# One power for queries and keys in two transformers, the first FFN's rounding done inside its attention, and a reordered layer norm after the recurrence

## The reference

```python
# layer 0, FFN: both operands of each product are rounded to FP4 in blocks of 16
scale = max(|xb|) / 6; scale = max(scale, 1e-12)
q = nearest_of_grid(xb / scale) * scale
gate = q(xn) @ q(w_gate).T ; up = q(xn) @ q(w_up).T
y = q(silu(gate) * up) @ q(w_down).T

# layers 2 and 3, FFN branch: a transformer of its own
# (layer 2: 6 layers, 16 heads, window 32; layer 3: 2 layers, 8 heads, window 64)
q = q / max(norm(q), 1e-12) * q_scale     # per head of 64, the same for k
q = rotate(q); k = rotate(k)
o = softmax(q k^T, banded) v
x = x + o @ wo ; x = x + w2(a * gelu(g)), a, g = split(w1(layernorm(shift(x))))

# layer 3, attention branch: a linear recurrence y, then
s = (y - mean) * rsqrt(var + eps) * gamma + beta
```

## Time and profile before

| | us |
|---|---|
| median of 3 runs | 4119.81 (4113.49 to 4121.21) |
| the profiled execution | 4123.83 |
| its span in the trace | 4122.1 |
| busy in the span: PE, DVE, ACT, POOL | 3719.1, 2877.2, 2448.5, 2308.0 |
| mean granted TensorE clock, share of full speed | 0.963 |

### The profile page before, as it was taken

How to read it: one execution, slowest core, us unless ns; L and a number is a source line. 1 busy time by engine, 2 the same in 40 slices (tenths; PEclk the granted TensorE clock), 3 DMA queues, 4 the chain that set the end, 5 groups by cost and what they waited for, 6 DMA issues and landing times. The chain is left out here.

```text
span 4122.1 us, 101183 instructions
## 1 busy us (share of the span) xinstructions
PE 3719.1 (90%) x40355; PEld 2527.8 (61%) x40365; DVE 2877.2 (70%) x6487; ACT 2448.5 (59%) x4999; POOL 2308.0 (56%) x2225
## 2 busy tenths in 40 slices
PE   7976999998999979999999999999999998768886
PEld 5554555544666646666666666666666666646665
DVE  3347454412666658888888888888888887558885
ACT  2223555523455557777767776777777776447775
POOL 1004000001111268888888888888888886257773
PEclk9997999998999989999999999999999999889998
DMA  0000000000000021112112112112111111120110
GB/s 20 2 8 23 1 1 1 6 24 7 2 2 2 2 79 41 41 41 67 41 41 67 41 41 67 41 41 67 41 41 38 41 41 33 34 69 23 24 24 19
DMA packets 103248, 128.53 MB, mean 31 GB/s; under 512 B 38232, under 2 KB 55680, under 8 KB 101888
## 3 DMA queue, kind: packets, MB, share of 16 engines
q1 hardware_dynamic: 102784, 122.05, 11.0%
HBM read 31.95 MB, written 3.54 MB: 9 GB/s over the span
## 5 line engine op out<-in xcount | busy, mean ns | idle before, releaser
L404 POOL TENSOR_TENSOR t_inv<-t_ssq,half 128x8 f32<-128x8 f32 x448 | 779.8, 1743 | 82.7 <-DVE t_ssq L682 62.5
L455 PE MATMUL t_wa<-t_w_qkv,t_resid 128*128 128x512 f32 x1344 | 694.4, 616 | 45.4 <-DMA t_scales<-in_L_ffn_k_scale 41.4
L415 POOL TENSOR_TENSOR t_ra<-t_qn,t_rot 128x512 f32<-128x512 f32 x448 | 570.3, 1273 | 85.1 <-DVE t_qn L689 76.7
L606 ACT ACTIVATE t_p<-t_p 128x384 f32<-128x384 f32 (+1 forms) x448 | 241.8, 540 | 331.2 <-DVE t_p L706 322.4
L715 DVE TENSOR_TENSOR t_ra<-t_ra,t_rb 128x512 f32<-128x512 f32 x448 | 311.0, 716 | 123.0 <-POOL t_rb L417 123.0
L484 PEld LDWEIGHTS t_T<-ident,t_p 128*96 128x96 f32 (+1 forms) x1792 | 193.1, 129 | 313.8 <-ACT t_p L606 280.4
L416 POOL TENSOR_TENSOR t_rb<-t_qn,t_rot 128x256 f32<-128x256 f32 x448 | 367.3, 820 | 0.0
L417 POOL TENSOR_TENSOR t_rb<-t_qn,t_rot 128x256 f32<-128x256 f32 x448 | 335.4, 749 | 0.0
L680 DVE TENSOR_REDUCE t_ssq<-t_sq 128x8 f32<-128x512 f32 x448 | 304.9, 681 | 12.0 <-ACT t_sq L598 8.2
L455 PEld LDWEIGHTS t_wa<-t_w_qkv,t_resid 128*128 128x128 f32 x1344 | 212.5, 192 | 163.2 <-issue 133.1
L492 PE MATMUL t_T<-ident,t_ra 128*128 128x128 f32 x1792 | 267.6, 277 | 44.0 <-ACT t_gg L645 32.4
(11 more groups left out here) (408 smaller groups left out, 8381.8 us busy)
## 6 DMA issues: line engine op xcount, KB each, us to landing
t_v<-t_vn SPq DMA_DIRECT2D x192, 198.0 KB, 2.6
t_v<-t_vn SPq DMA_DIRECT2D x248, 132.0 KB, 2.4
t_v<-t_vn SPq DMA_DIRECT2D x144, 66.0 KB, 1.9
t_w_qkv<-in_L_ffn_Wqkv SPq DMA_DIRECT2D x6, 1536.0 KB, 6.7
t_v<-t_nothing SPq DMA_DIRECT2D x48, 66.0 KB, 1.9
t_w_o<-in_L_ffn_Wo SPq DMA_DIRECT2D x6, 512.0 KB
f_h<-t_L_ffn_h_w SPq DMA_DIRECT2D x2, 1024.0 KB, 8.2
t_w<-in_L_ffn_W SPq DMA_DIRECT2D x6, 341.0 KB
```

The lines of the kernel that those rows point to most:

```text
L404: pool.tensor_tensor(inv[:, n % 2, r, :], ssq[:, n % 2, r, :], g["half"][:, 0:8], ALU.pow).then_inc(inved.sem, 1)
L415: pool.tensor_tensor(ra[:, n % 2, r], qn[:, r], spread(cos, 1, 8), ALU.mult).then_inc(cosd.sem, 1)
L455: pe.matmul(bank, resid[:, b, lo:lo + P], w_qkv[:, l % 2, at:at + 512], start=True, stop=True).then_inc(wa_up.sem, 1)
```

## The change

Three places. In `transformer` the floor and the power are done once for queries and keys, on 16 columns, after the keys' sums:

```diff
-        floored = st.event("floored", 2)
-        inved = st.event("inved", 2)
+        floored = st.event("floored")
+        inved = st.event("inved")
...
-                        for r in range(2):
-                            pool.wait_ge(floored.sem, floored.at(n, r + 1))
-                            pool.tensor_tensor(inv[:, n % 2, r, :], ssq[:, n % 2, r, :], g["half"][:, 0:8], ALU.pow).then_inc(inved.sem, 1)
+                        pool.wait_ge(floored.sem, floored.at(n))
+                        pool.tensor_tensor(inv[:, n % 2].rearrange("p r h -> p (r h)"), ssq[:, n % 2].rearrange("p r h -> p (r h)"), g["half"][:, 0:16],
+                                           ALU.pow).then_inc(inved.sem, 1)
...
                     v.tensor_reduce(ssq[:, n % 2, r, :], sq[:, r], X, ALU.add).then_inc(summed.sem, 1)
-                    v.wait_ge(summed.sem, summed.at(n, r + 1))
-                    v.tensor_scalar(ssq[:, n % 2, r, :], ssq[:, n % 2, r, :], 1e-24, None, ALU.max).then_inc(floored.sem, 1)
+                    if r:
+                        both = ssq[:, n % 2].rearrange("p r h -> p (r h)")
+                        v.wait_ge(summed.sem, summed.at(n, 2))
+                        v.tensor_scalar(both, both, 1e-24, None, ALU.max).then_inc(floored.sem, 1)
...
-                    v.wait_ge(inved.sem, inved.at(n, r + 1))
+                    v.wait_ge(inved.sem, inved.at(n))
```

```diff
+                    for k in ((0, 1, 2), (4, 5, 6))[half]:
+                        finish_rounding(k)
                     for b in range(NB):
+                        if half == 0 and b == 1:
+                            finish_rounding(3)
...
                             maxima(n + 2, 0)
+                            for i in range(PER_UNIT):
+                                round_step(PER_UNIT * (half * UNITS + n + 2) + i)
                             maxima(n + 2, 1)
...
-    parts = {"x0": (0, 512), "x1": (512, 512), "wgu": (WGU, 2 * NH * DIM), "wd": (WD, HID), "x2": (1024, 512), "x3": (1536, 512)}
-    for k in range(UNITS):
-        parts[f"h{k}"] = (HD + 2 * k * HID, 2 * HID)
...
-                for name, (lo, size) in parts.items():
+                for k in range(UNITS):
+                    lo, size = 2 * k * HID, 2 * HID
```

In `attention3`'s layer norm all four groups are measured first, their statistics counted four tiles ahead, and POOL takes the four powers in a row before the four additions of beta:

```diff
-                for i in range(T):
-                    v.bn_stats(stats[:, i, :], y[:, i, :]).then_inc(counted.sem, 1)
-                for k in range(6):
+                count_four(0)
+                for k in range(4):
+                    if k < 3:
+                        count_four(k + 1)
+                    measure(k)
+                for k in range(5):
                     if k < 4:
-                        measure(k)
-                    if 1 <= k < 5:
-                        shift(k - 1)
-                    if k >= 2:
-                        scale(k - 2)
+                        shift(k)
+                    if k:
+                        scale(k - 1)
```

More of the change, by code:

```diff
@@ L797, in attention0 @@
     loaded = early.loaded
-    wraw, wgraw, wv, wgv, wr, wo, gw, maskq, maskk, masklq, masklk = early.weights
+    wraw, wgraw, wv, wgv, wr, wo, gw, maskq, maskk, masklq, masklk, wff = early.weights
+    BL, HID, WGU = 16, 352, 3 * DIM
+    flat = lambda t, b: t[:, b * TPB:(b + 1) * TPB, :].rearrange("p t c -> p (t c)")
+    parts = [(flat(g["xn"], b), flat(g["u"], b)) for b in range(BATCH)]
+    parts += [(wff[:, lo:hi], wff[:, lo:hi]) for lo, hi in ((0, WGU), (WGU, 2 * WGU), (2 * WGU, 2 * WGU + HID))]
+    widths = [SEQ] * BATCH + [WGU, WGU, HID]
+    constants = flat(s, BATCH - 1)
+    blocks = lambda ap: ap.rearrange("p (k e) -> p k e", e=BL)
+    ROUND_STEPS, PER_UNIT = 7, 3
     with Stage(nc, "a0", early.sems) as st:
+        scale = st.sb("scale", [P, len(parts), SEQ // BL])
+        inverse = st.sb("inverse", [P, SEQ // BL])
+        r_stepped = st.sem("r_stepped")
+        r_lessened = st.sem("r_lessened")
         wqk = st.sb("wqk", [P, 2, G, 4, 32])
@@ L862, in _ @@
                 pool.memset(oE[:, :, :], 0.0)
-                pool.memset(oF[:, :, :], 0.0)
+                pool.memset(oF[:, :, :], 0.0).then_inc(zeroed, 1)
+                pool.wait_ge(zeroed, 12)
+                for k in range(2):
+                    pool.memset(wff[HID % P:P, (k + 1) * WGU - DIM:(k + 1) * WGU], 0.0)
             @block.sync
@@ L1309, in _, with ffn0 @@
                             gate_remote(b)
-def ffn0(nc, g, d):
+def ffn0(nc, g, early):
     HID, BL = 352, 16
@@ L3069, in program @@
                 ATTENTION[layer](nc, g, dram, early)
-            FFN[layer](nc, g, dram)
+                if layer == 0:
+                    ffn0(nc, g, early)
+            if layer > 0:
+                FFN[layer](nc, g, dram)
         between(nc, g, "end", True, out)
```

128 lines of the change are left out of this document (73 added, 55 removed).

## The result

The changed kernel takes 4248.57 us (median of 4 runs, 4247.01 to 4251.3), the kernel before 4120.51 us in the same rounds. The ratio is 1.0315, with a 95% interval of 1.0299 to 1.0332: slower by 3.2%. The profiled execution took 4249.49 us, its span is 4247.8 us. Against the 4123.8 us of the profiled execution before, that is 125.7 us more.

A forecast was written before the change was run, and what follows sets the result against it. It took the path between POOL and DVE in layer 2's transformer, half the run, as the bound. Terms 147 - 18 + 2 - 3 = +128 us on the 4119.8 us median gave 4248 us; own range 4220 to 4280, 8 in 10 within 4190 to 4285.

The forecast's parts named there:

- The wait: Layer 2's transformer: POOL stands idle from its run's end to the keys' floor, 1.64 us plus 0.07 us hand-over.
- The price of 16 columns: Layer 2's transformer: the merged power on POOL takes 2.88 us, estimated; bounds 1.64 and 3.28 us.
- Rivals 3 and 4: Merged power: 3, little cost beyond 8 columns, 4101 us, chance 0.04; 4, nothing shared, 3.28 us, 4325 us, chance 0.07.
- The ffn gap: Layer 2, between POOL's product runs in an ffn slot: 5.38 us replaces 4.15 us, +1.23 us.
- The tail gap: Layer 2, between POOL's product runs in a tail slot: 5.38 us replaces 5.53 us, -0.15 us.
- The second meeting: Layer 2: DVE's add of the queries meets rotary products in both runs, stretching the 5.25 us run to 5.70, +0.45 us.
- Rival 1: Layer 2's transformer: no new collision in the second run, +1.08 us per tile, 4205 us; chance 0.24.
- Layer 3: Layer 3's transformer: merged power ends before the variance's power, 0.6 us of cover left, 0 us for 32 slots.
- `ffn0`: Stage `ffn0`: PE can transpose at once after the rounding's move, so the first hidden part starts earlier, -18 us.
- `attention0`: Stage `attention0`: the rounding moved here is nearly all covered, +2 us, range 0 to 5.
- The norm: Stage `attention3`: ACT's waits between groups for POOL's powers go, the first group starts some 0.7 us later, -3 us.
- Rival 2: Layer 2's transformer: POOL's throughput decides, 0.40 us less in each of 192 slots, -77 us, 4024 us; chance 0.05.

The follow-up runs named there:

- split kernel: The changed kernel with floors and powers split again into two on 8 columns each, rounding and layer norm as changed: 4099.64 us, ratio 0.9939 to the kernel before.

## Why the prediction was right

It said 4248 us, and 4248.6 were measured. The mechanism held: the wait, the price and both gaps came out to 0.03 us. That the total did so too is in part luck. In layer 2, 7 us too much for the tiles met some 6 us of filling that I had left out; over the rest, +5.1 and +1.7 us against the forecast met -3.4, -3.4 and -2.0.

- **The wait.** 1.64 + 0.07 us were worked out from the earlier trace rows; POOL idles 1.68 us ahead of the power in the timeline above. The late floor costs nothing by itself: with a power of 1.65 us behind it, the gap is the old 4.14 us.
- **The price of 16 columns.** Estimated 2.88 us from the line through 1, 4 and 8 columns, measured 2.90. Rivals 3 and 4 fall with it.
- **The ffn gap.** +1.23 forecast, +1.25 measured. **The tail gap.** -0.15 forecast and measured.
- **The second meeting.** Forecast +0.45, measured +0.44 in that run, less 0.08 in the other, where the meeting was there already. Rival 1 falls. My reason was the missing floor and the later run together, with a floor of 0.21 us. In a tail slot of before that floor takes 0.63 us, since it begins under the run's last product, and that is what puts the addition at the end of the run. VectorE's timeline of before:

```profile
2503.49 0.63 DVE L682 TENSOR_SCALAR t_ssq<-t_ssq 128x8 f32<-128x8 f32 x1
```

Without the floor the addition begins 0.72 us ahead of the run's end instead of 0.06 (late power of 8 columns), together with the last product, and is the one that waits; the run stays at 5.25 us. With the longer ffn gap besides, it begins 1.67 us ahead, is running when the last product starts, and holds that up. So the missing floor alone is not enough. Whether the longer gap alone would be, with the floor in place, no run shows.
- **The tile and the total.** 1.46 us for 1.53, so 140 us over 96 tiles in place of 147. The stage still grew by 146.7, because of a term I did not have: the filling of the pipeline. The first two tiles took 18.49 and 19.44 us before, and 22.12 and 22.14 after, 3.4 us more than the usual difference, and the first products stand 2.1 us later behind the stage's start. In filling slots there is not yet other work that hides the wait.
- **Layer 3.** Forecast 0. The usual slot is 12.71 us as before, with cover left:

```profile
3997.37 2.91 POOL L403 TENSOR_TENSOR t_inv<-t_ssq,half 128x16 f32<-128x16 f32 x1 [3.11 <-DVE t_ssq L684]
4001.05 0.55 POOL L407 TENSOR_TENSOR t_rstd<-t_vare,half 128x1 f32<-128x1 f32 x1 [0.78 <-DVE t_vare L746]
```

The variance's power still waits 0.78 us behind the merged one; I had worked out 0.6. But the stretch grew by 5.1 us, of which 4.1 are its first four slots: 8.98, 9.86, 10.31 and 11.08 us before, 11.04 to 11.09 after, which is 5.69 + 5.38, a run and a gap with nothing else in the slot. The mis-sized term is again the filling.
- **`ffn0`.** Forecast -18, measured -20.0. TensorE's timeline, and VectorE's first hidden part, answer to the earlier trace rows:

```profile
295.20 1.09 PE L1474 MATMUL f_T<-ident,u 128*128 128x128 f32 x4 [4.47 <-PEq L61]
296.08 1.74 PE L1481 MATMUL f_T<-ident,w_wff 128*128 128x128 f32 x6
298.37 4.73 PE L1511 MATMUL f_G<-f_wguT,f_xqT 128*128 128x352 f32 x8 [0.55 <-ACT f_wguT L1569]
```

```profile
301.62 0.52 DVE L1441 TENSOR_TENSOR f_A<-f_sil,f_G 128x352 f32<-128x352 f32 x1 [16.34 <-ACT f_sil L1561]
```

The first product starts at 298.37 (I said 299.5), and the first hidden part 3.25 us behind it, for the 5.6 I had put in. I took the whole row of 4.92 us as what SiLU waits for, but the row groups eight matmuls, and the hidden part starts 1.5 us before the last of them ends. The -18 was too small by that, and 1.0 us was given back for the 0.8 of the forecast. TensorE's granted clock in the window of these 9 us (columns as in the earlier trace rows) is 0.52, the 1.2 GHz level. It was 0.50 already from 288 to 294 us, where TensorE was busy for 2.05 of 6 us. In the kernel before it was 0.50 from 294 to 315 us, where TensorE was busy for 2.4 of 21 us, and 0.67 from 315 to 325. The slow stretch ends 18 us sooner now (302.6 us for 320.4), as TensorE's dense work starts sooner:

```profile
294.00:303.00 9.00, 7.15 (x19) 4.58 (x20) 0.52 (x1) 3.26 (x5) 0.00 (x0) 0.52 0.01 2
303.00:360.00 57.00, 43.43 (x216) 32.12 (x214) 45.47 (x71) 19.05 (x45) 24.68 (x16) 0.86 0.00 1
```

- **`attention0`.** Forecast +2, measured -1.4 in the changed kernel and between -2.3 and +1.4 over all: covered, and 2 was too much.
- **The norm.** Forecast -3, measured -2.6 from the last mixing product to the transformer, and -2.3 against the kernel without it. The table's -1.3 is of a longer stretch, from layer 2's transformer on; it takes 142.5 to 149.5 us over the profiles, without order by the edits, and so says nothing of the norm. ScalarE's three groups of the earlier trace rows are one:

```profile
3760.46 5.73 ACT L2731 ACTIVATE a_gate<-a_Y,a_back,a_rstd 128x128 f32<-128x128 f32 x16 [11.92 <-DVE a_back L2810]
```

So with the real terms: 146.7 - 20.0 - 1.4 - 1.3 + 5.1 - 3.4 = 125.7 us for the 128 of the forecast.

**Rival 2**, that less work on POOL is a gain, is what the numbers of the page invite: 224 powers of 2.90 us for 448 of some 1.7. POOL's busy time in the stage did fall by 73 us, as that rival said (77). None of it reached the end. The Trainium skill (Perfetto Trace Analysis, "Optimizing Scalar/DVE Operations") says of ScalarE and VectorE that larger operations can help where the engine is saturated. Here POOL was 88% busy and still was not the one that ended the gaps; what ended them was the floor behind VectorE's keys' addition. With the floor early (keys' sum first), the merged power holds its own in layer 2, which is as near as these runs come to that rule.

## What to carry to other kernels

Merging two small operations saves their fixed cost (0.38 us of 3.28 here), but the merged one starts when the later input is there, and loses what the second covered. Add up lateness, price and what follows, and compare it with the gap that holds anyway: 1.68 + 1.65 + 0.81 cost nothing, 1.68 + 2.90 + 0.80, with the meeting that the longer gap brings, cost 149 us. And count the filling slots of a pipeline apart: there nothing covered the wait, and they cost some 10 us (3.4 + 2.1 + 4.1) that the period of the usual slots does not show.

## What the runs showed of the hardware

**An operation that starts while the other engine has one running waits for the rest of it, less 0.14 us.** This can be counted over the thirteen profiles for GpSimd's powers and products on one side and VectorE's additions and floors on the other. Where one starts with at least 0.2 us of the other left, it is longer than alone by what is left less 0.14 us. That holds to 0.01 us in all of 1222 powers and 884 products that start under an addition, and 693 additions and 697 floors that start under a product. Left out are pairs that start within 0.04 us of each other: there one waits and the other does not.

- A power. In the split kernel the first power of a tail slot starts at 2503.86 with 0.51 us of an addition left, and takes 2.01 us for 1.64. The timelines of POOL and VectorE, each with two operations in a row:

```profile
2503.86 3.64 POOL L404 TENSOR_TENSOR t_inv<-t_ssq,half 128x8 f32<-128x8 f32 x2
```

```profile
2503.69 1.29 DVE L715 TENSOR_TENSOR t_ra<-t_ra,t_rb 128x512 f32<-128x512 f32 x2
```

With the keys' sum first and the powers split, powers start with other rests: 0.60 us left makes them 0.46 longer, 0.41 makes 0.27, 0.32 makes 0.18, and 0.14 nothing. With the keys' sum first and 16 columns, 0.52 us are left and the power takes 3.28 us for 2.90.
- A product and an addition. In the changed kernel, above, the last product starts with 0.58 us of the addition left and takes 0.45 us more. That addition had started with 0.52 us of the product before it left and took 0.38 us more. The longest case has 1.11 us of a 128x512 product left, and the addition takes 1.66 us for 0.69 (split kernel, at 1477.27).

**A power under way holds nothing up.** An addition that starts beneath one keeps its 0.69 us. All 2041 that start with 0.2 to 2.9 us of a power left do, and 1111 floors keep their 0.17 us. The timelines of POOL and VectorE for one:

```profile
2514.94 1.65 POOL L404 TENSOR_TENSOR t_inv<-t_ssq,half 128x8 f32<-128x8 f32 x1
```

```profile
2515.45 0.69 DVE L715 TENSOR_TENSOR t_ra<-t_ra,t_rb 128x512 f32<-128x512 f32 x1 [1.06 <-POOL t_rb L417]
```

The Trainium skill (SBUF — State Buffer, "Who interferes with whom") says that whoever issues first has the shared ports for its whole instruction, and that the other is blocked. For products and additions, either way round, and for a power that starts second, the rows agree to the 0.14 us. For a power that starts first they do not, and the measurement decides.

What stays open: why a power under way lets an addition in where a product does not, where the 0.14 us come from, and why the layers that nobody edited take one of two times 3.5 us apart.
